# Graph attention on one core: f in four column groups, row 1's first chunk before row 0's second, strip 1's squares behind the exponentials

## The reference

```python
h = maximum(layernorm(x), 0)
g = inlayer2 @ W.T + b
f1 = g @ w1 + b1
f2 = g @ w2 + b2
logits = f1[:, None] + f2[None, :]
coefs = softmax(leaky_relu(logits, 0.01) + where(adj > 0, 0, -1e9), axis=-1)
out = x + coefs @ h
```

## Time and profile before

| | us |
|---|---|
| median of three runs | 1439.55 (1439.13 to 1439.86) |
| profiled execution, its own time | 1441.07 |
| its span | 1439.3 |
| PE busy | 1407.1 (98%) |
| DVE busy | 1276.7 (89%) |
| ACT busy | 614.6 (43%) |
| POOL busy | 264.2 (18%) |

### The profile page before, as it was taken

The page is one execution under the profiler, slowest core; times in us unless marked ns, Lnnn a source line. Parts: engine busy times, 40 slices in busy tenths (PEclk is TensorE's granted clock), DMA queues, the critical chain, the costliest instruction groups (busy, mean ns, idle before and its releaser), DMA issues.

```text
span 1439.3 us, 33339 instructions
## 1 busy us (share of the span) xinstructions
PE 1407.1 (98%) x12623; PEld 1246.2 (87%) x12623; DVE 1276.7 (89%) x1315; ACT 614.6 (43%) x713; POOL 264.2 (18%) x266
## 2 busy tenths in 40 slices
PE   8589999999999999999999999999999999999998
PEld 7468888888888888888888888888888888888887
DVE  5999989898898989989899898998989989898894
ACT  2895443444343444434444344443434434344330
POOL 0692011111110111111111011111101101111110
PEclk9799999999999999999999999999999999999999
DMA  9979999999999999999999999999999999999940
GB/s 293 322 178 217 233 232 234 233 224 212 211 211 207 217 209 209 215 208 210 210 215 210 208 215 209 210 216 208 210 208 217 210 209 216 207 212 212 211 106 12
DMA packets 110184, 302.43 MB, mean 210 GB/s; under 512 B 11732, under 2 KB 44628, under 8 KB 110164
## 3 DMA queue, kind: packets, MB, share of 16 engines
q1 hardware_dynamic: 100080, 289.52, 89.7%
q10 hardware_dynamic: 10084, 12.65, 3.0%
HBM read 293.73 MB, written 8.39 MB: 210 GB/s over the span
## 4 chain that ended last, share of the span: by engine, by line
PE 96%; DMA 2%; ACT 1%; DVE 1%; ACTq 0%; issue 0%; SPq 0%
PE acc L1055 62%; PE acc L1057 31%; PE rp L1010 2%; DMA adj_sb<-in_adj_dram 1%; ACT h_f L589 0%; ACT rp L573 0%; PE rp L1024 0%; DMA w<-in_L_gnn_w_dram 0%; PE small L997 0%; PE rp L1018 0%; DVE wgt L844 0%; ACT mask L573 0%; PE small L1069 0%; ACTq L343 0%; ACTq L348 0%
## 5 line engine op out<-in xcount | busy, mean ns | idle before, releaser
L1055 PE MATMUL acc<-H,wT 128*128 128x257 f16 x8192 | 1354.9, 273 | 9.2 <-DVE H L824 6.0
L1057 PE MATMUL acc<-H,wT 128*128 128x257 f16 x4096 | 1119.5, 273 | 0.0
L1055 PEld LDWEIGHTS acc<-H,wT 128*128 128x128 bf16 x8192 | 801.9, 98 | 110.9 <-issue 7.1
L854 DVE STREAM_TRANSPOSE wT<-wgt 128x1024 f32<-128x1024 f32 x512 | 634.7, 1241 | 130.2 <-PE acc L1057 130.1
L573 ACT ACTIVATE mask<-adj_sb 128x1024 bf16<-128x1024 int32 x504 | 521.2, 1055 | 535.4 <-DVE wgt L844 437.0
L844 DVE SCALAR_TENSOR_TENSOR wgt<-b_word,c_word,mask 128x1024 f32<-128x1024 f32 x504 | 627.4, 1257 | 1.0 <-ACT mask L573 1.0
L1057 PEld LDWEIGHTS acc<-H,wT 128*128 128x128 f16 x4096 | 401.6, 98 | 50.3
L493 POOL TENSOR_TENSOR x_res<-o_room,x_res 128x256 f32<-128x256 f32 x63 | 66.7, 1059 | 1099.4 <-ACT o_room L580 1073.1
L580 ACT ACTIVATE o_room<-acc,r_den 128x256 f32<-128x256 f32 x63 | 29.9, 475 | 236.6 <-DVE r_den L873 236.6
L498 POOL TENSOR_TENSOR o_room<-o_room,x_res 128x256 f32<-128x256 f32 x63 | 80.9, 1284 | 5.2
L495 POOL TENSOR_SCALAR o_room<-h_mean,no_nb 128x256 f32<-128x256 f32 x63 | 58.2, 924 | 0.0
(11 more groups left out here) (93 smaller groups left out, 162.4 us busy)
## 6 DMA issues: line engine op xcount, KB each, us to landing
adj_sb<-in_adj_dram SPq DMA_DIRECT2D x504, 512.0 KB, 8.6
x_res<-in_x_dram SPq DMA_DIRECT2D x64, 128.0 KB, 4.0
out_dram<-o_room SPq DMA_DIRECT2D x63, 128.0 KB, 4.3
H<-in_x_dram ACTq DMA_DIRECT2D x16, 256.0 KB, 12.7
H<-in_x_dram SPq DMA_DIRECT2D x16, 256.0 KB, 13.0
adj_sb<-in_adj_dram ACTq DMA_DIRECT2D x8, 512.0 KB, 14.7
wgt<-in_L_gnn_inlayer_dram ACTq DMA_DIRECT2D x8, 256.0 KB, 9.7
wgt<-in_L_gnn_inlayer_dram SPq DMA_DIRECT2D x8, 256.0 KB, 10.1
```

The costliest lines, as they stand in the source:

```text
L854: nc.vector.transpose(wT[:, wT_slot(I, k), :, :].rearrange("p t (g r) -> p g t r", g=Q), wgt[:, wgt_slot(I, c), :, s * SQ:(s + 1) * SQ]).t ...
L1055: pe.matmul(acc[:, par, 0:DV], w_hi[:, slot, t, :], H[:, j, part, 0:DV], start=(j == 0 and part == 0), stop=False)
L1057: mm = pe.matmul(acc[:, par, 0:DV], w_lo[:, slot, t, :], H[:, j, 0, 0:DV], start=False, stop=(j == ROWS - 1))
```

## The change

Parts of it:

- **f in column groups.** `V` has 32 weight columns instead of 128. The eight matmuls of a strip go to four groups of 32 PSUM partitions, two added up in each. What was one sum over eight is now four partial sums; after DVE's transpose, four small matmuls (`f_sums`) with `same` add the four groups. `chunk_f` is split into `chunk_turn` and `chunk_max` for this, and chunk 0's part moves in between the turns of strips 5, 6 and 7. Behind each `f_of_strip` but the last, PE gets `keep_busy(4)`: four fp32 matmuls of 128 columns whose result nobody reads.
- **ACT.** The second `f_to_sbuf` goes ahead of strip 1's sums. Strip 1's squares go behind the exponentials, and c's exponential ahead of them. The issues of x strips 6 and 7 come later; the two loads of chunks (row 1's chunk 0, then row 0's chunk 1) stand together behind `values(1)`.
- **Chunks.** Row 1's chunk 0 is loaded, masked and weighted ahead of row 0's chunk 1. PE takes (1,3) ahead of (0,4). Masks of row 0's chunk 1 go to SBUF and not to PSUM.
- **Unit 9's low part** moves from DVE to POOL.
- **DVE's** `raw_stats` near the maximum are moved behind it or between the packings of b; `rstds(2)` on POOL moves behind `affine(0)`.

The diff, cut to its core:

```diff
-        V = h_f32[:, 1, :, :].rearrange("p t d -> p (t d)").rearrange(
-            "p (m i) -> p m i", m=FM)
+        V = h_f32[:, 1, 0, :].rearrange("p (m i) -> p m i", m=FM)
...
+        low_on_pool = (0, 2, 4, 6, 8, 9, 10, 12, 14)
...
-            first_adj(sp, 1, (0, 1))
...
+                    if n == Q - 1 and is_row(I, 0):
+                        first_adj(sp, 1, (0, 1))
...
             low_of_values(8)
+            low_of_values(9)
             D_column(4)
             rstds(7)
             affine(7)
...
-                for m in range(FM):
-                    mm = pe.matmul(rp[:, k // SC, SQ * (k % SC):SQ * (k % SC + 1)], V[:, m, :], in2T[:, k % 2, m, :],
-                                   start=(m == 0), stop=(m == FM - 1))
+                for e in range(2):
+                    for g in range(Q):
+                        m = 2 * g + e
+                        mm = pe.matmul(rp[B * g:B * (g + 1), k // SC, SQ * (k % SC):SQ * (k % SC + 1)], V[:, m, :],
+                                       in2T[:, k % 2, m, :], start=(e == 0), stop=(e == 1))
                 mm.then_inc(f_done, 1)
+
+            def f_sums(c):
+
+                pe.wait_ge(f_cols_ready, c + 1)
+                pe.wait_ge(pick_ready, Q + 1)
+                parts = f_cols[:, c * CQ:(c + 1) * CQ].rearrange("p (j a o v) -> p a j o v", a=Q, o=2, v=Q)
+                for a in range(Q):
+                    mm = pe.matmul(f_sum_ps[B * a:B * (a + 1), c * ROWS:(c + 1) * ROWS], same[:, :],
+                                   parts[:, a, :, :, 0], start=True, stop=True)
+                mm.then_inc(f_sum_ps_ready, 1)
...
+            def keep_busy(n):
+                for _ in range(n):
+                    pe.matmul(acc[:, 0, 0:P], ones[:, :], ones[:, :], start=True, stop=True)
...
+            f_of_strip(5)
+            keep_busy(4)
+            f_sums(0)
+            f_of_strip(6)
+            keep_busy(4)
+            f_of_strip(7)
             pe.wait_ge(f2_of_ready, 1)
             b_exponents(0)
-
+            f_sums(1)
...
             products(1, 1, 2)
+            products(1, 1, 3)
             products(0, 0, 4)
-            products(1, 1, 3)
             products(0, 0, 5)
```

More of the change, by code:

```diff
@@ L139, in graph_attention @@
         F_ps = small[:, 1, 384:385]
+        f_sum_ps = small[:, 0, 256:256 + 2 * ROWS]
         hs_ps = small[:, 1, 0:D]
@@ L320, in wait_values, with wait_low @@
                 eng.wait_ge(h_ready, HALF * (n - before + 1))
+        low_on_pool = (0, 2, 4, 6, 8, 9, 10, 12, 14)
+        def wait_low(eng, n):
+            before = sum(m < n for m in low_on_pool)
+            if n in low_on_pool:
+                eng.wait_ge(lo_ready, before + 1)
+            else:
+                eng.wait_ge(lo_dve_ready, n - before + 1)
         def wait_slot(eng, n):
@@ L571, in mask_part @@
                 act.wait_ge(adj_loaded[c], 16 * Q * (I + 1))
-                place = row0_mask[c][g] if is_row(I, 0) else mask[:, c, g * CQ:(g + 1) * CQ]
+                place = row0_mask[g] if is_row(I, 0) and c == 0 else mask[:, c, g * CQ:(g + 1) * CQ]
                 nc.scalar.activation(place, adj_sb[:, c, g * CQ:(g + 1) * CQ], ACT.Relu,
@@ L626, in _ @@
             load_x(act, 4, 5, (2, 3))
-            sums(1)
             f_to_sbuf(1)
             load_x(act, 5, 6, (2, 3))
-            squares(1)
-            load_x(act, 6, 7, (2, 3))
+            sums(1)
             act.wait_ge(f2_rel_ready, 1)
@@ L637, in _ @@
             b_of_chunk(1)
-            load_x(act, 7, 8, (2, 3))
-            values(0)
             act.wait_ge(t_ps_ready, 1)
@@ L643, in _ @@
                                  ACT.Exp).then_inc(c_exp, 1)
+            squares(1)
+            load_x(act, 6, 7, (2, 3))
+            values(0)
             high_of_values(0)
@@ L794, in variance @@
                                         ALU.add).then_inc(var_ready, 1)
-            for k in range(2, NS):
-                turn_in2(k)
-            chunk_f(0)
+            turn_in2(2)
+            turn_in2(3)
+            turn_in2(4)
+            turn_in2(5)
+            chunk_turn(0)
+            turn_in2(6)
+            chunk_max(0)
+            turn_in2(7)
+            chunk_turn(1)
+            chunk_max(1)
             raw_stats(16, 20)
-            chunk_f(1)
-            raw_stats(20, 24)
             dve.wait_ge(u_ready, Q + 1)
@@ L842, in weights @@
                     dve.wait_ge(t_ready, nth_strip(0, 7))
-                shown = row0_mask[c][g] if is_row(I, 0) else mask[:, c, g * CQ:(g + 1) * CQ]
+                shown = row0_mask[g] if is_row(I, 0) and c == 0 else mask[:, c, g * CQ:(g + 1) * CQ]
                 nc.vector.scalar_tensor_tensor(out=wgt[:, wgt_slot(I, c), g, :], in0=b_word[:, c * CQ:(c + 1) * CQ],
@@ L910, in _ @@
             turn(1, 0)
+            weights(0, 0, 1)
+            turn(1, 1)
+            weights(0, 1, 1)
+            turn(1, 2)
+            raw_stats(60, 64)
+            variance(7)
             weights(0, 2, 1)
-            turn(1, 1)
+            turn(1, 3)
             weights(0, 3, 1)
-            turn(1, 2)
-            low_of_values(9)
             turn(0, 4)
-            turn(1, 3)
             low_of_values(11)
+            turn(0, 5)
             weights(1, 0, 1)
-            turn(0, 5)
             weights(1, 1, 1)
@@ L1025, in _ @@
             pe.wait_ge(u_ready, Q)
-            for k in range(NS):
-                f_of_strip(k)
+            f_of_strip(0)
+            keep_busy(4)
+            f_of_strip(1)
+            keep_busy(4)
+            f_of_strip(2)
+            keep_busy(4)
+            f_of_strip(3)
+            keep_busy(4)
+            f_of_strip(4)
+            keep_busy(4)
+            f_of_strip(5)
+            keep_busy(4)
+            f_sums(0)
+            f_of_strip(6)
+            keep_busy(4)
+            f_of_strip(7)
             pe.wait_ge(f2_of_ready, 1)
             b_exponents(0)
+            f_sums(1)
             pe.wait_ge(ident_ready, 1)
@@ L1048, in products @@
                     wait_high(pe, 2 * k + 1)
-                    for part in (lo_ready, lo_dve_ready, D_column_ready):
-                        pe.wait_ge(part, k + 1)
+                    wait_low(pe, 2 * k)
+                    wait_low(pe, 2 * k + 1)
+                    pe.wait_ge(D_column_ready, k + 1)
                 slot = wT_slot(I, k)
```

88 lines of the change are left out of this document (43 added, 45 removed).

## The result

Timed side by side on one chip, the changed kernel took 1447.35 us, median of 5 runs (1445.85 to 1448.87), and the kernel before 1439.86 us (1439.13 to 1441.16). The ratio is 1.0051, with a 95% interval of 1.0040 to 1.0062. The change costs 7.5 us. The forecast was 1440.8, in a range up to 1443.7: it was wrong. The profiled execution of the changed kernel took 1447.35 us with a span of 1445.6, 6.3 us more than the 1439.3 of before.

What follows compares the result with a forecast made beforehand. PE, busy 98%, was taken as the bound, so its last stall sets the end. Earlier f was given back by squares; POOL's column then moved (1,4) by +1.3 us: 1440.8 us, 8-in-10 range 1437.5 to 1443.7.

Steps and rivals of the forecast that it cites:

- The marker: Start of (1,4), row 1's strip 4, at 107.72 us before; nothing waited behind it; predicted to move by +1.3 us.
- f: PE's first matmuls, now in column groups: end taken as 39.4 us, where it was 41.96 before.
- the four-way case: In f on PE, fp32 matmuls overlap across four groups: 0.9 us a strip, f ends at 38.8, `keep_busy` costs nothing.
- Rival (a): f overlaps only in pairs, ending at 41.3: 1442.7 us; PE's new wait costing the clock adds up to 1.6; chance 0.22.
- from f to the masks: c's exponential 12.0 us after f, at 51.4; then squares, 4.0 us, delay ACT: first mask 58.7, first weights 59.7.
- row 1's first turn: On DVE, starts at 87.7 against 88.00; the DMA wait goes, ACT is late instead, and PE does not wait.
- the four issues: Loads of the matrix issued by ACT behind values(1): 1.6 us, less 0.5 of the last value.
- the longest of ACT's three waits in the sum: ACT ahead of row 1's first chunk: 1.0 us, counted with 0.4 and 0.8 as DMA wait that goes.
- PE at (1,0): PE reaches row 1's first strip at 88.9 us without a wait and is not slow there, worth 1.6 us.
- POOL's D column of strip 5: Done at 105.3 with unit 9's 2.14 us added; PE waits for it from 102.1, ahead of (0,5).
- DVE's turn for (1,4): Takes 20.9 us from 87.7 to 108.6, just ahead of (1,4) at 109.0, so POOL sets the time.
- the clock behind the marker: A slow strip after PE's new wait, adding up to 1.6 us; with the forecast's own f, up to 1442.4 us.

Runs made afterwards that it cites:

- the last experiment: Changed kernel plus eight full-width fp32 matmuls that nobody reads, in PE's wait ahead of (1,4); 1445.38 us, ratio 1.0036.
- the first experiment: Kernel before plus only the f and ACT part, with the old order of chunks and unit 9's low part on DVE; 1444.21 us, ratio 1.0025.
- the pair that differs in two masks: Changed kernel with spread squares, no `keep_busy`, strip 7's statistics and variance moved; masks (0,2,1) and (0,3,1) in PSUM 1441.07 us, in SBUF 1443.16.

## Why the prediction was wrong

The marker was right as a measure. In all fourteen profiles the span is the start of (1,4) plus 1331.5 to 1331.6 us, or plus 1333.3 where the clock fell there (the changed kernel, the one with the order of chunks alone, the variance on POOL, and no `keep_busy`).

**Right, f.** Predicted: between 38.8 and 40, 39.4 taken. Measured 39.81. A strip takes 1.07 us, close to the four-way case (0.9), and `keep_busy` 1.16 instead of 1.7. Rival (a)'s pairs (1.9) don't exist; a strip of 1.93 is one at half clock.

**Right, from f to the masks.** c's exponential ends at 51.4 (51.4), first weights at 59.28 (59.7). The terms: `f_sums` 0.41 (0.9 taken), b's second exponent 3.78 at low clock (3.4), c's matmuls 1.81 (2.0). The squares do give back what f won. The low clock behind f, which the sum took, isn't the same in every execution: that of the last experiment had full clock there. And in the old order of chunks the same ACT work is a loss: the first experiment is 3 to 4 us slower by its median, of which 2.6 are the squares.

**Right by number, row 1's first turn:** 87.75 (87.7), without a wait of PE. Two errors cancel. ACT was 2 us earlier than taken at unit 7's high part (79.1 against 81.1); 1.6 of them are the four issues, which cost ACT nothing: they lie beside its values. DVE lost that again, in the two weights of 4.34, which alone take 2.5. One reading was wrong without an effect: the longest of ACT's three waits in the sum (1.0, at 84.39) isn't for a DMA. The chain of waits of the kernel before has two issues of ACT there, 0.37 us at 83.43 and 0.45 at 83.84. It went as well, since the values stand beside the issues now.

**Wrong without an effect, PE at (1,0):** 90.78 (88.9). The slow strip that the sum struck out came one strip earlier, at (0,3), behind its wait of 2.70 us. DVE was later still.

**Right by number, POOL's D column of strip 5:** 105.0 (105.3). It is luck: the stretch begins at 78.14 and not at 80.2, and takes 26.9 us instead of 25.1, since POOL is held by DVE too. And it wasn't what PE waited for.

**Wrong, the step that failed:** "DVE's turn for (1,4) took from 88.00 to 106.5; now two weights and a statistic more and one low part less, 20.9, so 87.7 + 20.9 = 108.6, just ahead. POOL sets the time." From 87.75 to the turn's end at 112.2 it took 24.5 us. The variance took 2.87, where it took 0.17 in the kernel with masks in SBUF, 2.7 more, and unit 11's low part 2.48, 0.7 more than the 1.76 of before. Together 3.4 of the 3.6 that are missing. Durations of the kernel before were added up for instructions that now stand beside others on POOL, as if engines waited only for semaphores. The experiment with masks in SBUF in the kernel before, and the pair that differs in two masks, show the mechanism in both directions (+2.4 and -2.1 us), on other instructions than these two. The section on the change had named the edit, masks of row 0's chunk 1 to SBUF, and the sum had no term for it at all. In the profile of the changed kernel those four weights are not held themselves (1.24 to 1.27 us). They hold POOL, whose values beside one of them take 3.24 us at 90.21 instead of 2.18; and where the variance was taken out of their way, one of them was held in its place, 3.98 us. The rows of before had a sign of it: the earlier trace rows has a copy of 128 x 16 at 1.26 us beside that low part of 1.76, and another copy at 0.26.

**Wrong, the clock behind the marker.** Rival (a) had this price, at up to 1.6 us and for my wait of 3 us ahead of (0,5). It came ahead of (1,4): 1.7 us. Five kernels have a wait of 2.44 or 2.45 us there. The clock fell behind it in four and stayed at 1.00 in the one with unit 9's low part on DVE, so the length of the wait doesn't decide it. What does decide it stays open.

**How the 7.5 us are made up.** By parts, from the ratios: the f and ACT part 0.0025 x 1440 = 3.6, the order of chunks with its masks in SBUF 3.0 (the masks alone 0.0015 x 1440 = 2.2), and unit 9 on POOL (1.0051 - 1.0037) 2.0, together 8.6; they overlap, and by the intervals each is uncertain by 1.3 us or more. By the profile: DVE's stretch is 24.5 - 18.5 = 6.0 longer, of which 2.4 were in the sum as work moved there and 3.4 are holds; it begins 0.25 earlier, and in the kernel before DVE was 1.2 ahead of PE at its end. 6.0 - 0.25 - 1.2 = 4.6 at the marker, and 1.7 of clock. This is an account of two executions. The remaining 1.2 between 6.3 in the spans and 7.5 in the medians is how the two profiled executions lie among their runs (that of before was 1.2 above its median).

## What to carry to other kernels

Before adding up durations, look what runs on GpSimd at the same time: an instruction of VectorE with two operands in SBUF isn't the same instruction beside a GpSimd one. An edit that moves an operand from PSUM to SBUF, or work from VectorE to GpSimd, needs a term of its own for that, and so does a load that is issued later behind work thought to be hidden. A duration several times its usual one, with no bracket, is a wait that the profile counts as work. And before two profiles are compared, compare the durations and the clock in a stretch where the programs are the same.
